# Sixteen constant products around the eight turns of each normalisation

## The reference

```
def _layernorm(x, axis=-1, eps=1e-05):
    m = jnp.mean(x, axis=axis, keepdims=True)
    v = jnp.var(x, axis=axis, keepdims=True)
    return (x - m) / jnp.sqrt(v + eps)
...
x = x + _L0_xattn_ref(_layernorm(x), side, ctx, ctx, ...)   # cross-attention over 4096 context tokens
x = x + _L0_attn_ref(_layernorm(x), ...)                    # self-attention, 16 heads
x = x + _L0_ffn_ref(_layernorm(x), ...)                     # shared and routed experts
x = x + _L1_xattn_ref(_layernorm(x), ctx, ctx, ...)         # cross-attention
x = x + _L1_attn_ref(_layernorm(x), ...)                    # two kinds of scores
x = x + _L1_ffn_ref(_layernorm(x), ...)                     # token-shifted feed-forward
x = x + _L2_xattn_ref(_layernorm(x), ctx, ...)              # low-rank attention
x = x + _L2_attn_ref(_layernorm(x), ...)                    # state space scan
x = x + _L2_ffn_ref(_layernorm(x), ...)                     # experts that choose tokens
x = x + _L3_xattn_ref(_layernorm(x), ctx, ...)              # has an RMS norm of its own
x = x + _L3_attn_ref(_layernorm(x), ...)
x = x + _L3_ffn_ref(_layernorm(x), ...)                     # has two RMS norms of its own
```

## Time and profile before

| | us |
|---|---|
| three timed runs | 2756.80, 2743.03, 2754.75 |
| their median | 2754.75 |
| the profiled execution | 2750.46 |
| its span, first to last instruction | 2748.6 |

### The profile page before, as it was taken

The page is one execution under the profiler, slowest core; times in us unless marked ns, Lnnn a source line. Parts: engine busy times, 40 slices in busy tenths (PEclk is TensorE's granted clock), DMA queues, the critical chain, the costliest instruction groups (busy, mean ns, idle before and its releaser), DMA issues. The chain is left out here.

```text
span 2748.6 us, 38678 instructions
## 1 busy us (share of the span) xinstructions
PE 2333.9 (85%) x15024; PEld 1363.0 (50%) x15024; DVE 1455.3 (53%) x2285; ACT 1055.1 (38%) x1896; POOL 380.9 (14%) x659
## 2 busy tenths in 40 slices
PE   3999999868999698999996684886889799697778
PEld 1344444435699463454443443352238557364447
DVE  4777777423221356888883684225877332223333
ACT  2566666512111233777774371123432133021310
POOL 2453000000000400000001250001630000000100
PEclk8899999978899897999998777886989899898889
DMA  7977543020353698556430001001004430200200
GB/s 192 237 183 160 119 90 58 12 96 1 138 229 140 221 281 244 108 93 127 93 59 34 12 1 59 28 1 63 0 19 166 168 123 1 96 1 2 99 1 8
DMA packets 108213, 258.59 MB, mean 94 GB/s; under 512 B 11808, under 2 KB 83072, under 8 KB 94080
## 3 DMA queue, kind: packets, MB, share of 16 engines
q1 hardware_dynamic: 101696, 203.71, 28.2%
q0 software_dynamic: 2736, 39.37, 4.2%
q10 hardware_dynamic: 3600, 13.04, 1.2%
HBM read 211.26 MB, written 44.83 MB: 93 GB/s over the span
## 5 line engine op out<-in xcount | busy, mean ns | idle before, releaser
L666 DVE TENSOR_REDUCE sta_parts<-sta_psA 128x1 f32<-128x1024 f32 x544 | 625.6, 1187 | 188.6 <-PE sta_psA L583 186.8
L724 ACT ACTIVATE sta_probs<-sta_psS 128x512 f32<-128x512 f32 x1056 | 575.8, 597 | 274.9 <-PE sta_psS L594 272.8
L594 PE MATMUL sta_psS<-L_xattn_qS,L_xattn_kst 99*128 99x256 bf16 x2112 | 356.3, 278 | 11.5 <-ACT sta_probs L724 6.6
L583 PE MATMUL sta_psA<-L_xattn_kst,L_xattn_qS 99*128 99x512 bf16 x1088 | 293.3, 387 | 46.9 <-PEq L59 32.1
L594 PEld LDWEIGHTS sta_psS<-L_xattn_qS,L_xattn_kst 99*128 99x128 bf16 x2112 | 161.4, 98 | 259.5 <-ACT sta_probs L724 183.3
L603 PE MATMUL sta_psO<-sta_probs,L_xattna_V 128*32 128x256 f32 x2560 | 189.5, 385 | 0.0
L583 PEld LDWEIGHTS sta_psA<-L_xattn_kst,L_xattn_qS 99*128 99x128 bf16 x1088 | 104.3, 99 | 131.7 <-DVE sta_parts L666 43.7
L202 ACT ACT_TABLE_LOAD x14 | 18.0, 1283 | 327.7 <-PEq L59 327.7
L603 PE MATMUL sta_psO<-sta_probs,L_xattn_V 128*32 128x256 f32 x1536 | 114.8, 390 | 0.0
L1008 ACT ACTIVATE sht_probs<-sht_psS 128x768 f32<-128x768 f32 (+1 forms) x64 | 55.3, 863 | 148.8 <-PE sht_psS L852 99.7
L443 POOL CAST sta_split<-sta_neg 128x2 bf16<-128x2 f32 x64 | 12.1, 188 | 715.9 <-issue 467.5
(11 more groups left out here) (625 smaller groups left out, 3922.4 us busy)
## 6 DMA issues: line engine op xcount, KB each, us to landing
L_xattn_kst<-L_xattn_keys SPq DMA_DIRECT2D x186, 136.0 KB, 5.1
L_xattn_kst<-L_xattn_keys SPq DMA_DIRECT2D x186, 128.0 KB, 4.6
L_xattn_values<-prj_rows SPq DMA_DIRECT2D x64, 256.0 KB, 3.7
L_xattn_keys<-prj_parts SPq DMA_DIRECT2D x32, 384.0 KB, 4.0
L_xattna_V<-in_ctxV SPq DMA_DIRECT2D x5, 2048.0 KB, 11.9
L_xattna_V<-L_xattn_values SPq DMA_DIRECT2D x5, 2048.0 KB, 11.1
l2f_W<-in_M SPq DMA_DIRECT2D x10, 1024.0 KB, 7.6
L_xattn_keys<-sta_bparts SPq DMA_DIRECT2D x24, 384.0 KB, 7.1
```

The lines of the kernel that those rows point to most:

```text
L583: last = nc.tensor.matmul(psA[:, u % 2, col:col + rhs.shape[1]], lhsT, rhs, start=True, stop=True)
L594: last = nc.tensor.matmul(psS[:, at % 2, j * T:(j + 1) * T], lhsT, rhs, start=True, stop=True)
L666: nc.vector.tensor_reduce(into(parts[:, u // n % 2]), view(psA[:, u % 2, :]), AX.X, ALU.max).then_inc(max_taken, 1)
L724: nc.scalar.activation(probs[:, u % NP, i * 512:(i + 1) * 512], psS[:, at % 2, :], ACT.Exp, scale=scale).then_inc(probs_ready, 1)
```

## The change

`normalize` gets a further PSUM tile `psI` of one bank and an argument `fill`, true unless said otherwise. With it, TensorE multiplies the bf16 identity by the 128 x 512 bf16 mask into `psI` ten times ahead of its first wait for `rows_ready`, and six times more behind the last transpose. Nothing reads `psI`, and the sixteen products raise no semaphore. The first call, before which the bf16 constants are not there, is made with `fill=False`. So 13 calls issue sixteen matmuls and sixteen weight loads more each.

```
-def normalize(nc, K, X, xn, xnT, eps, rms=False, w=None):
+def normalize(nc, K, X, xn, xnT, eps, rms=False, w=None, fill=True):
...
         psT = p.ps("psT", [P, KC, 512])
+        psI = p.ps("psI", [P, 512])
...
                 if xnT is None:
                     return
+                for _ in range(10 if fill else 0):
+                    nc.tensor.matmul(psI[:], K["ident16"], K["mask16_q"], start=True, stop=True)
                 for t in range(NT):
                     pe.wait_ge(rows_ready, t + 1)
                     for k in range(KC):
                         last = nc.tensor.transpose(psT[:, k, t * P:(t + 1) * P], xn[:, t, k * P:(k + 1) * P], K["ident"])
                 last.then_inc(turned, 1)
+                for _ in range(6 if fill else 0):
+                    nc.tensor.matmul(psI[:], K["ident16"], K["mask16_q"], start=True, stop=True)
...
-                normalize(nc, K, X, xn, xnT, 1e-5)
+                normalize(nc, K, X, xn, xnT, 1e-5, fill=False)
```

## The result

| | before | changed |
|---|---|---|
| median of 20 runs, us | 2749.36 | 2731.07 |
| lowest to highest | 2737.91 to 2756.80 | 2726.32 to 2743.47 |
| ratio, 95% interval | | 0.9944 (0.9930 to 0.9957) |
| span of the profiled execution | 2748.6 | 2727.5 |
| mean granted clock | 0.895 | 0.913 |

The changed kernel is 0.56% faster, 15.4 us by the ratio (the medians lie 18.3 apart). The forecast was 9.3 us and "within 0.5%" as the likeliest, and whether 0.56% is inside or outside of that the interval does not decide. Its time of 2743 was against a median of 2754.75 from three runs, which 20 runs put at 2749.4. The two profiles lie 21 us apart, more than the runs do: the changed kernel's twenty runs fall into twelve from 2726.3 to 2732.5 us, with a mean granted clock of 0.912 to 0.915, and eight from 2735.7 to 2743.5 with 0.908 or 0.909, and its profile (2729.3) is of the first group.

A forecast was written before the change was run, and what follows sets the result against it. TensorE, busy 85% of the span, runs at 1.2 GHz behind normalisations where VectorE is the chain and TensorE idles. Costs 6.6 + 3.3 less gains 19.2 gave -9.3 us; forecast 2743, range 2727 to 2766.

The forecast's parts named there:

- within 0.5%: Whole kernel: a change within 13.8 us, about what a measurement can tell from no change; chance 0.52.
- The cost of the products: At 13 normalisations: the sixteen products add 6.6 us at six calls starting at 1.2 GHz and 3.3 at seven others.
- the slow starts: Six calls starting at 1.2 GHz, `l0a` to `l3a`: +1.1 us each, +6.6 together, bounds 2.4 and 10.8.
- the seven others: `l0f`, `l1f`, `l2s`, `l2f`, `l3f_xn`, `l3x_zn`, `l3f_x`: products cost +3.3 us together, bounds 2 and 13.
- The clock's rise: At calls starting at 1.2 GHz: identity-times-mask products lift TensorE's clock 3.2 to 6.0 us after the first statistic.
- rival 3: All 13 calls: the constant product doesn't lift the clock, or too late; +31 us, 2783, milder form 2767; chance 0.13.
- Rival 1: Behind the normalisations: the clock holds over the gaps too, all time at 1.2 GHz comes back; about -21, 2731; chance 0.25.
- the own case of 4 to 15: Whole kernel: the forecast's central case, going from -4 to -15 us; chance 0.48.
- one chance in three: Stage behind `l0a`: odds that the clock holds over some 2.4 us of idle TensorE; 0.9 of 2.7 us counted.
- the 1.7 us at the first product: Behind `l2s`: gain while VectorE waits for TensorE's first product, counting only the first 3.8 us at 1.2 GHz.
- The penalty formula: Twelve stretches behind normalisations: time at slow clock times one minus the ratio, 30.7 us; with costs -21, 2731.
- a shift of over 3 us far from a normalisation: Stages far from a normalisation: a shift this large would mean something not in the sum decides.

The follow-up runs named there:

- experiment 1: The changed kernel with the sixteen products reading one row of identity and mask instead of 128; 2787.4 us, ratio 1.0140 to the kernel before.
- experiment 7: The changed kernel with products only at l0a, the second L_xattnq, l1b, l2x, l3x_xn, l3x_zn and l3a; ratio 0.9937 to the kernel before.
- experiments 2 to 8: Changed kernel with 10 ahead/0 behind: 0.9949; 0/6: 1.0031; 10/3: 0.9949; products at `l2s` only: 1.0013; six calls starting at 2.4 GHz: 0.9983; seven remaining: 0.9937; gaps filled: 0.9929.

## Why the prediction was right, and where not

The profiles of one form can be grouped. The stretch from each normalisation's first statistic to the next's, in profiles without and with ten and six products at that call, beside what was summed for it:

| call | without, us | with, us | difference of means | summed |
|---|---|---|---|---|
| `l0a` | 115.7 to 115.9 (5) | 112.3 to 112.4 (3) | -3.5 | +0.2 |
| `l0f` | 239.3 to 239.7 (5) | 236.2 to 236.5 (3) | -3.0 | -1.9 |
| second `L_xattnq` | 580.9 to 584.7 (5) | 580.5 to 581.0 (3) | -3.0 | -0.9 |
| `l1b` | 168.9 to 169.3 (5) | 169.2 to 169.4 (3) | +0.2 | -0.5 |
| `l1f` | 40.7 to 42.5 (5) | 40.9 to 41.2 (3) | 0 | +0.1 |
| `l2x` | 136.8 to 142.4 (5) | 135.0 to 135.1 (3) | -4.7 | -2.0 |
| `l2s` | 185.2 to 192.2 (3) | 183.2 to 185.1 (3) | -4.8 | -1.6 |
| `l2f` | 129.3 to 132.1 (5) | 129.5 to 130.2 (3) | -0.6 | -0.7 |
| `l3x_xn` and `l3x_zn` | 178.3 to 178.9 (5) | 176.9 to 177.7 (3) | -1.4 | +0.9 |
| `l3a` | 145.4 to 146.5 (5) | 143.5 to 146.9 (3) | -0.3 | -0.9 |
| `l3f_xn` | 114.9 to 115.8 (5) | 115.1 (3) | 0 | -2.0 |
| `l3f_x` | 120.1 to 120.5 (5) | 120.3 to 120.8 (3) | +0.2 | 0 |

- **The cost of the products** held in kind and was summed too high. At 2.4 GHz: nothing ahead, 0.57 behind. At the slow starts the next work came 0.2 (`L_xattnq`), 0.3 (`l3x_xn`), 0.5 (`l0a`), 0.6 (`l3a`), 0.7 (`l2x`) and 1.7 us (`l1b`) later; the clock rose at S+2.8 to S+3.8 in the first five and at S+6.0 in `l1b`. That is 4.0 us where 6.6 was summed, because five of six rises came at S+3.8 or sooner, two of them ahead of the span of 3.2 to 6.0 that I gave them. At the seven others it is 2.4 (1.3 of it at `l3f_x`, where the clock fell while TensorE followed VectorE's pace) where 3.3 was summed. So 6.4 in this profile against 9.9.
- **The clock's rise** held. Products of identity and mask lift it as other whole work does; rival 3's mechanism came only with one-row products (experiment 1). Its price of 31 us was 38: I had the seven other calls pay 1.8 each, and they paid 1.8 to 2.8, the six slow ones 3.3 instead of 3.05.
- **Rival 1** (the clock holds over the gaps too) was right for `l0a`, the two RMS calls and most of `l0f` and wrong for `l1f`, as forecast there. The 15.4 lies just outside the own case of 4 to 15 and short of that rival's 21.
- **`l0a`** was mis-sized by the odds. I gave the clock one chance in three to hold over the cast stage; with six behind it held in each of the three profiles. The 2.7 us were won, and in the attention behind it one fall lasted 3.4 us instead of 6.8.
- **`l0f`**: the sixteen logit products took 1.9 us as forecast, and the clock, which had been down for 13.7 us from S+3.6, was down for 3.4 from S+10.6. More than the 0.6 that I gave the next stage came back.
- **The second `L_xattnq` and `l2x`** were mis-sized in kind: I counted only the first stretch at 1.2 GHz. Before, TensorE waited 4.87 us for `prj_rows` until 970.8, and the clock fell in that wait, at 969.2, and stayed down for 6.8 us; now TensorE comes one batch further before it waits, and the clock is down for 3.4:

Kernel before, TensorE at that wait, and the clock behind it:

```profile
970.81 3.78 PE L1170 MATMUL prj_psV<-L_xattn_L_xattn_weights,L_xattnq_cxT 128*128 128x256 f32 x8 [4.87 <-DVE prj_rows L1210]
```

```profile
970.00:976.00 6.00, 5.19 (x10) 0.50 1.09 347
```

Changed kernel, the same wait, and the clock behind it:

```profile
971.00 3.31 PE L1176 MATMUL prj_psV<-L_xattn_L_xattn_weights,L_xattnq_cxT 128*128 128x256 f32 x8 [4.06 <-DVE prj_rows L1216]
```

```profile
970.00:976.00 6.00, 5.00 (x12) 0.72 1.12 361
```

  The kernel with products at the fast starts alone also had the short form there (580.9), so it is not tied to the products at this call. In `l2x` the first stretch at 1.2 GHz lasted 8.4 us where I counted 6.2 (3.1 of gain), and from S+96 on the clock was down for 20.5 us in the one profile of the kernel before and 30.7 in the other, and for 17.1 in each of the three with products.
- **`l3f_xn`, `l3a` and `l1b`** were mis-sized the other way. The starts ran at 2.4 GHz, and DVE's first copy in `l3f_xn`'s stage came 1.5 us earlier against the normalisation, but at the next one nothing was left. In `l3a`'s attention the clock was down for 17 us in one piece in the changed profile, and for 6.8 before. In experiment 7, with the same products at `l3a`, it was down for 3.4 there, and the stretch was 143.5 instead of 146.9. `l1b`'s gain of 1.6 went into its own late rise.
- **`l2s`**: the 1.7 us at the first product are there, but the products at this call alone did not make the kernel faster. The stretch scatters between 183 and 192 us with where the clock stands in the small stages and in the scan.
- **The penalty formula** of "TensorE: Matmul & The Clock Gate" in the Trainium skill, section Terms, taken over the twelve stretches, gave 30.7 us of gain and with my costs -21. The measured 15.4 lies between that and my 9.3. Over the whole profile the time at 1.2 GHz fell by 105 us; the formula would make 53 us of it, and the profiles differ by 21. So the traces do not bear it out where other engines end the waits.

So the direction, the mechanism and the range stood. What was too small is the sum: the costs were 3.5 us too high, and gains that I took to end with the first stretch go on in stages further down, while two that I took as safe were lost there. That the sum misses by only 6 us is partly luck, since such errors partly cancel: by the table it has 3.7 us too little at `l0a` and 2.0 too much at `l3f_xn`. The prediction named a shift of over 3 us far from a normalisation as the sign of something outside its sum, and that sign came: the scan behind `l2s` was 4.5 us shorter in the changed profile (122.7 to 118.2). That these later falls differ is shown; that any one of them is caused by the products at a given call is not. For the stretch of a call as a whole it is shown where every profile with the products is under every one without: `l0a` (by 3.3 us or more), `l0f` (2.8), `l2x` (1.7) and, narrowly, the `l3x` pair (0.5).

## What to carry to other kernels

Where TensorE idles for some microseconds ahead of each of many short stages, products whose result nobody reads are worth trying, if they are whole (all rows) and end before the data they precede: ahead they were free at 2.4 GHz and held the turns up by as much as 1.2 us where the clock was still at 1.2, and behind they cost what outlasts the last copy. Sum such a change from each stage's start, but expect the gain at a start to be kept, doubled or lost by later falls of the clock, and measure parts of it over many runs: one pair of profiles showed 9 us at a place where the products alone made the kernel no faster.

## What was not expected of the hardware

- Sixteen products of one row and 512 columns kept TensorE as busy as whole ones, ten in 4.42 us, and left the clock at 1.2 GHz; the granted clock behind them was 0.57 to 0.77 as without them.
- The kernel before scatters by 0.7% (2737.9 to 2756.8) with nothing changed. In its two profiles the state space sublayer took 192.2 and 190.3 us, in the changed kernel and those of experiments 2 to 8 it took 183 to 191, and the scan within it took 118.2 us at a mean clock of 0.97 (changed kernel) and 124.1 at 0.88 (experiment 1).
